# First units of an additive attention on half of the keys, and the key and query products of the first tokens moved ahead of the last round's transposes

## The reference

```python
# 1: neighbourhood attention, 7x7 window, 8 heads of 16, bias rpb; gate; then a normalisation
attn = einsum('bijnd,bijnpqd->bijnpq', q * hd**-0.5, k[window]) + rpb
out  = (softmax(attn) @ v[window]) @ proj_w + proj_b
y    = x + out * sigmoid(relu(x @ g1_w + g1_b) @ g2_w + g2_b)
t    = layernorm(y) * ln_g + ln_b
# 2: additive attention inside each image, 32 hidden units, on n = layernorm(t)
h    = tanh((n @ Wt)[:, i, None, :] + (n @ Wx)[:, None, j, :] + bh)
t    = t + softmax(h @ Wa + ba) @ n
# 3: top-1 mixture of 8 experts (128 -> 512 -> 128) on layernorm(t), with capacity 320
t    = t + expert(layernorm(t))
```

## Time and profile before

| | us |
|---|---|
| median of 3 runs | 670.28 (670.21 to 670.32) |
| profiled execution, its time | 668.23 |
| its span | 666.4 |
| ACT busy | 578.6 (87%) |
| PE busy | 540.0 (81%) |
| DVE busy | 487.6 (73%) |
| POOL busy | 484.2 (73%) |

### The profile page before, as it was taken

One profiled execution on the slowest core, in us unless ns is written; L12 is line 12 of the kernel. 1 busy time (PEld: TensorE's weight loads), 2 busy tenths in 40 slices (PEclk: granted clock), 3 DMA queues, 4 the chain that ended last, 5 costly groups with the idle time before them and its releaser, 6 DMA issues.

```text
span 666.4 us, 12523 instructions
## 1 busy us (share of the span) xinstructions
PE 540.0 (81%) x4580; PEld 270.4 (41%) x4580; DVE 487.6 (73%) x1381; ACT 578.6 (87%) x416; POOL 484.2 (73%) x584
## 2 busy tenths in 40 slices
PE   9999879998989889986877867676686767787992
PEld 6666533343444344443322312222131222357872
DVE  4777667869897977786678987687868768732466
ACT  4777599999999999999999999999999999950540
POOL 1004688978989768969989998888889888710565
PEclk9999998999999889999988999999989999997998
DMA  8700100000000000006200000000000000003300
GB/s 316 238 1 2 64 1 25 40 1 5 10 5 10 5 0 15 10 5 245 100 0 13 14 1 13 10 5 9 4 13 1 13 8 6 11 4 92 85 23 32
DMA packets 14108, 24.32 MB, mean 36 GB/s; under 512 B 1296, under 2 KB 11058, under 8 KB 13024
## 3 DMA queue, kind: packets, MB, share of 16 engines
...
...
## 4 chain that ended last, share of the span: by engine, by line
PE 32%; issue 22%; ACT 21%; DVE 18%; POOL 5%; DVEq 0%; POOLq 0%; ACTq 0%
ACT front L1247 18%; PE ps L959 7%; DVE front L1536 3%; PE ps L750 3%; PE ps L1127 3%; POOL front L623 3%; PE ps L1131 3%; PE ps L798 2%; PE ps L779 2%; PE ps L996 2%; PE ps L1019 2%; DVE back L1351 2%; DVE back L1378 1%; PE ps L789 1%; POOL x_one L600 1%
## 5 line engine op out<-in xcount | busy, mean ns | idle before, releaser
L1247 ACT ACTIVATE front<-front 128x4096 f32<-128x4096 f32 (+1 forms) x125 | 418.5, 3394 | 1.3 <-POOL front L623 0.7
L623 POOL TENSOR_SCALAR front<-k,q 128x1024 f32<-128x1024 f32 (+1 forms) x424 | 387.0, 930 | 44.7 <-PE ps L959 36.9
L959 PE MATMUL ps<-front,cst 128*32 128x512 f32 x2032 | 254.2, 621 | 72.6 <-ACT front L1247 65.6
L1536 DVE TENSOR_SCALAR front<-ps,q 128x512 f32<-128x512 f32 x218 | 188.3, 902 | 19.9 <-PE ps L959 16.6
L959 PEld LDWEIGHTS ps<-front,cst 128*32 128x32 f32 x2032 | 55.3, 112 | 188.2 <-issue 97.6
L1173 ACT ACTIVATE back<-back,mn 128x320 f32<-128x320 f32 (+1 forms) x128 | 62.6, 540 | 9.6 <-DVE mn L1351 9.6
L1351 DVE CUSTOM_DVE_ANT_0 back<-ps,back 128x320 f32<-128x320 f32 (+1 forms) x128 | 54.0, 469 | 10.3 <-PE ps L750 8.9
L1568 DVE COPY ptm<-ps 128x512 f32<-128x512 f32 x31 | 21.4, 691 | 37.6 <-PE ps L985 35.9
L1235 ACT ACTIVATE front<-k,q 128x1024 f32<-128x1024 f32 (+1 forms) x50 | 45.9, 950 | 2.0 <-DVE k L1638 2.0
L570 POOL TENSOR_TENSOR lnw<-lny,lnh 128x4 f32<-128x4 f32 (+1 forms) x9 | 1.8, 197 | 57.1 <-DVEq L1511 51.8
L750 PE MATMUL ps<-conv 32*128 32x320 f32 (+1 forms) x256 | 38.4, 472 | 1.6 <-DVE mn L1351 1.3
...
...
## 6 DMA issues: line engine op xcount, KB each, us to landing
back<-in_w SPq DMA_DIRECT2D x2, 2048.0 KB, 11.0
...
```

What stands on the lines that cost most here:

```text
L623: last = nc.gpsimd.tensor_scalar(ring[u % DEPTH][:, at + lo:at + hi], k4[:, img * L + k0 + lo:img * L + k0 + hi], q4[:, m:m + 1], 1.0, ALU ...
L959: last = nc.tensor.matmul(bank(to)[c * U:(c + 1) * U, :], c_("wa", U - QPG - QPG * row, 2 * U - QPG - QPG * row), ring[t % DEPTH][:, at:at ...
L1247: last = nc.scalar.activation(ring[t % DEPTH][:, 0:to], ring[t % DEPTH][:, 0:to], ACT.Tanh)
L1536: last = nc.vector.tensor_scalar(ring[u % DEPTH][:, at + lo:at + keys], ps[:, base + k0 + lo:base + k0 + keys], q4[:, m:m + 1], None, ALU.add)
```

## The change

1. `GROUPS`: blocks 0 and 1 both go by halves, in the order block 0 and block 1 over the first 512 keys (units 0 to 7), then block 0 and block 1 over the last 512 (units 8 to 15). The second half of the keys is first used in unit 8, where it was unit 4 (`NEW_KEYS`, `KEYS_NEEDED`). DVE sums from unit 8 on, where it was unit 5. Only unit 0 is all ACT's own (`BIASED`); in units 1 to 7 POOL forms five or six of the eight tiles and ACT takes three or two with the bias. Block 0 ends with unit 11 instead of 7.
2. Order before stage 2: on PE the query columns and the key product of the first tokens stand in front of round 15's project, values and transposes, and the token transposes in front of the sums of round 14; ACT copies the tokens between two exponentials of round 15, and copies round 15's chunk 0 after the first tile of unit 0 and the heads after the third; DVE copies the keys first in round 15, and takes the second statistics of blocks 0 to 3 in round 11 instead of 12.
3. POOL's row scalings use `add` of a negated mean (`mvn`, `negm`, each written by one small DVE instruction) in place of `subtract` of the mean.
4. The rounds of image 2, the value rows, the entry of the last query and key rows, and the tokens and keys of image 2 stand two steps later; the second tokens of image 1 follow at step 3 instead of 1.

```diff
-BEGIN = dict(zip(range(RS, NR), [2, 4] + [6 + 3 * k for k in range(12)] + [42, 44]))
-ROWS_STEPS = (3, 4, 5)
-ENTRY = 8
-KEYS_1, TOKENS_2, KEYS_2 = 1, 50, 51
+BEGIN = dict(zip(range(RS, NR), [4, 6] + [8 + 3 * k for k in range(12)] + [44, 46]))
+ROWS_STEPS = (5, 6, 7)
+ENTRY = 10
+KEYS_1, TOKENS_2, KEYS_2 = 3, 52, 53
...
-GROUPS = [Group(0, 0, 0, CH // 2), Group(0, 1, CH // 2, CH // 2)] + [Group(p, None, CH * p, CH) for p in range(1, NB)]
-NEW_KEYS = [0, CH // 2, T // 2]
-BIASED = (0, CH // 2)
+GROUPS = [Group(n % 2, n // 2, n * CH // 2, CH // 2) for n in range(4)] + [Group(p, None, CH * p, CH) for p in range(2, NB)]
+NEW_KEYS = [0, CH, T // 2]
+BIASED = (0,)
 HEAVY = range(36, T // 2)
...
     gate = lambda u: KEYS_1 if u < NEW_KEYS[2] else project_step(NB - 1) + 6
-    return [u for u in range(NEW_KEYS[1] + 1, T) if max(u - DEPTH + 1, gate(u)) == t]
+    return [u for u in range(NEW_KEYS[1], T) if max(u - DEPTH + 1, gate(u)) == t]
...
-    return 0 if u in BIASED else 6 if u < NEW_KEYS[1] else 3 if u in HEAVY else 8
+    return 0 if u in BIASED else 6 - u % 2 if u < NEW_KEYS[1] else 3 if u in HEAVY else 8
...
-    return max(0, u - NEW_KEYS[1])
+    return max(0, u + 1 - NEW_KEYS[1])
...
         g1 = pm[:, 0:L // 2]
-        pmh = sb("pmh", [P, 1, HL])
-        nmh = sb("nmh", [P, 1])
+        pmh = sb("pmh", [P, 2, HL])
+        nmh = sb("nmh", [P, 2])
         nml = sb("nml", [P, 1])
...
         mvs = sb("mvs", [P, NB, 2])
+        mvn = sb("mvn", [P, NB])
+        negm = sb("negm", [P, 1])
         lnh = sb("lnh", [P, NB])
...
-        KEYS_NEEDED = {BIASED[0] + 1: 1, BIASED[1] + 1: 2, T // 2: 4}
+        KEYS_NEEDED = {1: 1, NEW_KEYS[1]: 2, NEW_KEYS[2]: 4}
...
                 for j in range(lo, hi):
-                    last = nc.gpsimd.tensor_scalar(y_all[:, j, :], y_all[:, j, :], mvs[:, j, 0:1], lny[:, j:j + 1],
-                                                   ALU.subtract, ALU.mult)
+                    last = nc.gpsimd.tensor_scalar(y_all[:, j, :], y_all[:, j, :], mvn[:, j:j + 1], lny[:, j:j + 1],
+                                                   ALU.add, ALU.mult)
                 chain(last)
...
                 for j in range(lo, hi):
-                    last = nc.gpsimd.tensor_scalar(x_all[:, j, :], y_all[:, j, :], mvs[:, j, 0:1], lny[:, j:j + 1],
-                                                   ALU.subtract, ALU.mult)
+                    last = nc.gpsimd.tensor_scalar(x_all[:, j, :], y_all[:, j, :], mvn[:, j:j + 1], lny[:, j:j + 1],
+                                                   ALU.add, ALU.mult)
                 last.then_inc(t_ready[lo // 4], 1)
...
                 pool.wait_ge(sy_ready, p + 1)
-                nc.gpsimd.tensor_scalar(r[:, 0:C], r[:, C:2 * C], mv[:, 0:1], sy[:, :], ALU.subtract,
-                                        ALU.mult).then_inc(xn_ready, 1)
+                nc.gpsimd.tensor_scalar(r[:, 0:C], r[:, C:2 * C], negm[:, :], sy[:, :], ALU.add, ALU.mult).then_inc(xn_ready, 1)
...
-            key_query_sums(1)
-            key_query_sums(2)
-            normal_rows(2, 4, 6)
-            key_query_sums(3)
+            for u in range(1, NEW_KEYS[1]):
+                if u == 4:
+                    normal_rows(2, 4, 6)
+                key_query_sums(u)
             for t in range(KEYS_1, END):
...
                     scores(rho + 1)
+                else:
+                    pe.wait_ge(n_ready, NG * RS)
+                    query_columns(0, 1)
+                    key_half(0, 2)
                 if rho >= 3 and rho % 2:
...
                 turn_probs(rho, 0)
+                if rho == RS - 2:
+                    pe.wait_ge(n_ready, NG * (RS - 1) + 1)
+                    turn_tokens(0, 0)
                 if rho >= 2 and rho % 2 == 0:
                     sums((rho - 2) // 2)
                 turn_probs(rho, 1)
-                if rho == RS - 2:
-                    pe.wait_ge(n_ready, NG * (RS - 1) + 1)
-                    turn_tokens(0, 0)
                 if rho >= 2 and rho % 2 == 0:
...
-            pe.wait_ge(n_ready, NG * RS)
-            query_columns(0, 1)
             values(RS - 1)
-            key_half(0, 2)
             sums(BS - 1)
...
                     soften(rho + 1, (0, 1))
-                turned(rho, 0)
+                if rho + 1 < RS:
+                    turned(rho, 0)
+                if rho == RS - 2:
+                    tokens_out(0, 0)
                 if rho + 1 < RS:
                     soften(rho + 1, (2, 3))
-                if rho == RS - 2:
-                    tokens_out(0, 0)
                 if CHUNKS[kind_of(rho // 2)] > 2:
...
             nc.scalar.activation(q4[:, 0:P], bank(1, 0, P), ACT.Identity, bias=c_("bh")).then_inc(q4_ready, 1)
-            heads_out(BS - 1)
...
                         act.wait_ge(h_used, t - DEPTH + 1)
-                    for at, k0, keys, m, _, _ in tiles[own:]:
+                    for n, (at, k0, keys, m, _, _) in enumerate(tiles[own:]):
+                        if t == 0 and n == 1:
+                            turned(RS - 1, 0)
+                        if t == 0 and n == 3:
+                            heads_out(BS - 1)
                         last = nc.scalar.activation(ring[t % DEPTH][:, at:at + keys], k4[:, k0:k0 + keys], ACT.Tanh,
...
                 a = slice(lo, hi)
+                nc.vector.tensor_scalar(mvn[:, a], mvs[:, a, 0], -1.0, None, ALU.mult)
                 link(nc.vector.tensor_scalar(half, mvs[:, a, 1], 1e-5, 0.5, ALU.add, ALU.mult))
...
                 a = slice(lo, hi)
+                nc.vector.tensor_scalar(mvn[:, a], mvs[:, a, 0], -1.0, None, ALU.mult)
                 link(nc.vector.tensor_scalar(lnh[:, a], mvs[:, a, 1], 1e-5, 0.5, ALU.add, ALU.mult))
...
             value_rows(2, 6)
+            def keys_out(half, frm):
+                dve.wait_ge(k4_done, half + 1)
+                nc.vector.tensor_copy(k4[:, half * 512:(half + 1) * 512], bank(frm)).then_inc(k4_ready, 1)
+
             for rho in range(RS):
                 j = (rho - 2) // 2
+                if rho == RS - 1:
+                    keys_out(0, 2)
                 if rho + 1 < RS:
...
                     link.end()
-                if rho == 12:
+                if rho == 11:
                     dve.wait_ge(ln_rows, 1)
...
                 link(nc.vector.bn_aggr(mv[:, :], stats[:, :]))
+                nc.vector.tensor_scalar(negm[:, :], mv[:, 0:1], -1.0, None, ALU.mult)
                 link(nc.vector.tensor_scalar(sv[:, :], mv[:, 1:2], 1e-5, 0.5, ALU.add, ALU.mult))
...
-            def keys_out(half, frm):
-                dve.wait_ge(k4_done, half + 1)
-                nc.vector.tensor_copy(k4[:, half * 512:(half + 1) * 512], bank(frm)).then_inc(k4_ready, 1)
-
-            keys_out(0, 2)
             inverse(BS - 1)
```

## The result

The kernel after takes 682.22 us (679.29 to 684.34, 6 runs), that of before beside it 670.33 (670.21 to 670.47): a ratio of 1.0177, 95% interval 1.0154 to 1.02. It is slower by 12 us where 2 us faster was predicted. The profiled execution took 684.34 us, with a span of 682.2.

A forecast was written before the change was run, and what follows sets the result against it. ACT, hardly resting from 83 to 586 us, was taken as the bound. Head -1.65, key wait -0.66, tiles +0.85, exponentials +0.2, idle time -0.9, tail +0.2 give -1.96: from 670.28 to 668.3 us, range 667.3 to 669.4.

The forecast's parts named there:

- (a): POOL's 128x128 row scaling with add and multiply: 0.44 us instead of 0.787, so 0.35 saved each.
- (b): Head, second statistics in round 11 instead of 12: round 15's scores come about 1.0 to 1.3 us late, at 74.95.
- (c): New order before the last transposes: keys copied 79.2 to 79.9, first tanh at about 79.9, 3.1 us earlier.
- (d): Two ACT copies moved behind the first and third tile: 0.85 us in ACT's stream, plus waits of 0.25 each.
- The head: Everything up to image 2's first tile: a gain of 1.65 us, with bounds of 0.5 and 2.7.
- First eight units: The wait for the second key half goes, -0.66 us; ACT's extra tiles add 0.85, block 1's halved exponentials 0.2.
- Rounds two units later: Image 2's rounds, under ACT until unit 55: ACT's work unchanged, 0.9 of 1.2 us of idle time gone.
- ACT's gap at 322.50: In the kernel before, ACT idle 0.66 us for POOL, late there from rows to scale and chains of statistics.
- a stall of 0.1 us: Before unit 64: with PE as late as before, POOL's sums end at 356.6 us, when ACT wants them at 356.5.
- The rival with 2.2 us at this place: POOL no faster with add, so ACT stands 2.2 us before unit 64; 672.7 us in all, chance 0.16.
- the third: POOL faster, but the two units' delay creates as much idle time at units 47 to 64 as it removes; 669.5 us, chance 0.14.
- Tail: After 586 us, the added negated mean in the last block's chain is on the path: +0.2 us.

The follow-up runs named there:

- fill: The kernel after with 24 and 14 products that nobody reads on PE, ahead of its waits in steps 48 and 53; 677.64 us, ratio 1.0113.
- apart_after: The kernel after with block 1's closing work two steps later, nothing else; 677.26 us, ratio 1.0102.
- shift_only: The kernel before with image 2's rounds, value rows, entry and tokens two steps later, nothing else; 676.62 us, ratio 1.0139.
- add_only: The kernel before with POOL's row scalings as add of a negated mean, nothing else; 669.81 us, ratio 1.0011.
- copy_first: The kernel after with DVE's statistics of six blocks behind the chunk copy of step 47 instead of ahead of it; 680.43 us, ratio 1.0158.

## Why the prediction was wrong

**POOL's row (a)**: right, 0.449 us against 0.44.

**Statistics in round 11 (b)**: DVE's wait to 63.64 (63.3), round 13 at 66.07 (65.85) and round 14 at 70.12 (69.8) are within 0.35 us; the price passed on to round 15 was mis-sized: 76.50 where I had 74.95. The 1.0 to 1.3 us that I carried through the round became 2.8, for a stretch at half clock was in no term. From the statistics to round 15's scores after takes 12.9 us and fill, whose clock stayed up there, 11.3; I had 11.65. But fill has its half clock at 85 us instead, and its head gains nothing either.

**Tokens and keys (c), copies in the stream (d)**: the order is as described, the key copy ended at 81.55 instead of 79.9, the copies behind tiles one and three waited 0.15 and 0 (0.25 each), image 2's copy ended at 90.06 instead of 88.0. The head gained -0.3 us, where 1.65 was the forecast and 0.5 my lower bound.

**First eight units**: right. No wait at unit 8, eighteen tiles in units 1 to 7 as counted, 2.33 for the 2,560-wide tanh less 0.1 of overlap, as worked out. Unit 8 began at 119.48, 2.0 us behind the 117.5 forecast, which is the head's shortfall. What I left out comes later: I asked only whether ACT, POOL and DVE were in time, never what it does to PE and DVE that two blocks now close together in steps 14 to 28. apart_after puts 5 us of the 12 on that.

**Rounds two units later**: this is the step that failed. I wrote that all the work is the same, "ACT's sum does not change", and took 0.9 of 1.2 us of idle time as gone. It is the same work, but it meets the closings of the blocks, which stay on their grid of eight steps, at other places of the queue. Where I had -0.9 us, shift_only measured +7.7, and units 48 to 64 show 6.1 us of it net of moved work. The reading that the term rests on was wrong too. I put ACT's gap at 322.50 down to POOL's rows, but PE was late there. In before, POOL's sums for it start only when PE's energies are done, and these stood behind a wait of PE for DVE's chain:

```profile
314.19 0.58 PE L822 MATMUL ps<-cst,ots 128*128 128x4 f32 x4 [4.08 <-DVEq L1457]
...
316.67 2.78 PE L959 MATMUL ps<-front,cst 128*32 128x512 f32 x16
```

```profile
319.60 2.88 POOL L623 TENSOR_SCALAR front<-k,q 128x1024 f32<-128x1024 f32 x3 [0.52 <-PE ps L959]
```

So faster rows had nothing to give there, as add_only shows, and PE had no slack left (a lag of 10.0 and 10.4 us) when the shift added to it. copy_first shows one of the new meetings: the statistics chain ahead of the chunk copy, which made 6.16 us of wait. A second is unit 64: I forecast a stall of 0.1 us, and it was 1.92 in after. I had reckoned with keys two units later and PE as late as before; but PE waited 3.35 us for DVE's chain up to 359.91, in step 59, and DVE copied the keys only at 368.00. The rival with 2.2 us at this place had the size by luck, for a reason that wasn't there (POOL's rows were fast). What of the 6.1 us lies in each of the other waits, between 327 and 345 us, I did not separate.

**The rivals**: the third had the mechanism, "statistics of step 46 in front of block 5's minimum at 48", and a price of 0.9 us. It priced the chain as one late minimum, and not by the lag that it leaves: after unit 48 the lag shrinks by about 1 us a unit (12.7, 11.3, 10.3, 9.4, 9.2), and at unit 53 the next wait comes on top. In after the slow clock adds to both.

**Tail**: the negated mean is in the chain, too small to tell.

How the 12 us divide: 5 go when block 1's closing moves away from block 0's, and some 4.6 when idle products keep the clock up in steps 48 and 53; the waits themselves stay. These two were measured by edits that add up. The last 3 or so are only what is left over, and the shift's later keys and statistics and a head that gains nothing are my guess at them. It is a division of the way back from after, and not one by the parts of the change: shift and halves cost 8 to 9 us each when alone, and why the fill gives 4.6 us on after and nothing clear on shift_only stays open.
